# Two expert tiles per step, and TensorE's float32 work in six groups per turn

## The reference

```python
# 1 causal linear attention (4 heads of 64, 128 features), then a ReLU network
q, k = heads(x @ Wq) * dh**-.25, heads(x @ Wk) * dh**-.25; v = heads(x @ Wv)
qp, kp = phi(q), phi(k)          # exp(x@omega.T - |x|^2/2 - max)/sqrt(128) + 1e-6
attn = causal(qp @ kp.T) @ v / (row sums) @ Wo
h = layernorm_1e6(x + attn);  out = relu(h @ W1 + b1) @ W2 + b2      # 256 -> 1024 -> 256
# 2 cross attention, one head of 256, on a context of 256 rows
out = softmax((x@Wq.T + bq) @ (c@Wk.T + bk).T / 16) @ (c@Wv.T + bv)
# 3 mixture of experts: 16 experts, the best 2 for each row
gates = top2 of softmax(x @ Wg.T), normalised
out = sum_e gates[:, e] * ((silu(x @ W1[e]) * (x @ W3[e])) @ W2[e])     # 256 -> 176 -> 256
```

## Time and profile before

| | |
|---|---|
| median of 3 runs | 808.99 us (808.33 to 810.88) |
| the profiled execution | 809.31 us, of it 807.5 us from the first to the last instruction |
| PE / PEld busy | 98% / 93% of the span |
| DVE / ACT / POOL busy | 73% / 54% / 49% |
| turns 4 to 14 (the loop) | 143.25 to 546.00 us, 36.6 us each |
| tile stage | from 634.1 us (first row transpose) to the end |

### The profile page before, as it was taken

The page is one execution under the profiler, slowest core; times in us unless marked ns, Lnnn a source line. Parts: engine busy times, 40 slices in busy tenths (PEclk is TensorE's granted clock), DMA queues, the critical chain, the costliest instruction groups (busy, mean ns, idle before and its releaser), DMA issues. The chain is left out here.

```text
span 807.5 us, 20968 instructions
## 1 busy us (share of the span) xinstructions
PE 789.9 (98%) x5911; PEld 750.1 (93%) x5912; DVE 592.1 (73%) x1720; ACT 435.1 (54%) x1193; POOL 393.6 (49%) x560
## 2 busy tenths in 40 slices
PE   9999999999999999999999999999999999999995
PEld 8899999999999999999999999999897899999994
DVE  4757777888787878878887878778767566666663
ACT  4473554637273554547372644546255377767773
POOL 2432134443545344544445344544436368687886
PEclk9999999999999999999999999999999999999998
DMA  9786673755747392846657382849779458777780
GB/s 270 255 285 235 211 263 102 268 178 191 246 162 272 108 314 82 286 147 220 217 173 263 127 306 91 294 135 346 253 299 353 138 107 132 121 127 130 132 140 2
DMA packets 105962, 161.19 MB, mean 200 GB/s; under 512 B 10705, under 2 KB 69649, under 8 KB 105041
## 3 DMA queue, kind: packets, MB, share of 16 engines
q1 hardware_dynamic: 80544, 132.89, 48.0%
q0 software_dynamic: 14800, 17.61, 11.9%
q10 hardware_dynamic: 10576, 10.19, 4.9%
HBM read 50.14 MB, written 112.47 MB: 201 GB/s over the span
## 5 line engine op out<-in xcount | busy, mean ns | idle before, releaser
L799 POOL DMA_INDIRECT out<-narrow,sidx x79 | 122.8, 1554 | 45.4 <-DVE sidx L2043 23.3
L1274 ACT ACTIVATE xn3T<-ps 128x512 f32<-128x512 f32 (+1 forms) x18 | 10.3, 574 | 140.4 <-PE ps L819 135.9
L808 PE MATMUL ps<-w_hi,fT_hi 128*128 128x256 f32 x256 | 79.8, 312 | 0.2
L1339 ACT ACTIVATE phi<-ps,nmax 128x128 f32<-128x128 f32 x256 | 73.5, 380 | 8.1 <-DVE nmax L1745 7.9
L1601 DVE TENSOR_TENSOR fT_lo<-relu_v,fT_hi 128x512 fp32r<-128x512 f32 x64 | 51.1, 798 | 32.3 <-ACT relu_v L1353 32.3
L808 PE MATMUL ps<-w_hi,fT_lo 128*128 128x256 f32 x256 | 72.3, 282 | 0.0
L808 PE MATMUL ps<-w_lo,fT_hi 128*128 128x256 f32 x256 | 72.1, 282 | 0.0
L1353 ACT ACTIVATE relu_v<-ps,b_sb 128x256 f32<-128x256 f32 x128 | 68.9, 538 | 0.0
L1352 ACT ACTIVATE fT_hi<-ps,b_sb 128x256 fp32r<-128x256 f32 x128 | 67.9, 530 | 1.0 <-PE ps L808 1.0
L808 PE MATMUL ps<-hT_hi,w_hi 128*128 128x256 f32 x256 | 67.1, 284 | 0.0
L808 PE MATMUL ps<-hT_hi,w_lo 128*128 128x256 f32 x256 | 66.9, 283 | 0.0
(11 more groups left out here) (330 smaller groups left out, 2715.1 us busy)
## 6 DMA issues: line engine op xcount, KB each, us to landing
expert_rows<-zero_rows SPq DMA_DIRECT2D x16, 4352.0 KB, 16.2
narrow<-expert_rows ACTq DMA_DIRECT2D x71, 136.0 KB
expert_up_hi<-X SPq DMA_DIRECT2D x16, 352.0 KB, 2.8
e_hi<-expert_up_hi SPq DMA_DIRECT2D x2, 2816.0 KB, 10.1
part_raw<-in_E SPq DMA_DIRECT2D x30, 176.0 KB
expert_up_lo<-part_raw SPq DMA_DIRECT2D x15, 352.0 KB, 3.1
e_lo<-expert_up_lo SPq DMA_DIRECT2D x2, 2464.0 KB, 13.0
X<-in_x SPq DMA_DIRECT2D x16, 256.0 KB
```

Of the source, the lines that this page charges most:

```text
L799: pool.indirect_dma_start(out_rows, bass.IndirectOffsetOnAxis(sidx[:, u:u + 1], 0), yg[:, u, :], None, bounds_check=NT * P - 1, oob_is_err ...
L808: return pe.matmul(out_, lhsT, rhs, start=start, stop=stop)
L1274: return act.activation(out_, in_, ACT.Copy)
L1339: last = act.activation(phi[:, g, h, :], ps[:, g, h * M:(h + 1) * M], ACT.Exp, bias=nmax[:, g, h:h + 1])
```

## The change

In the turns: both halves of the q projection come first; context values are made in two halves around the transposes of xn2 (now into bank 2) and y, which thus stand together; `by_feature` waits first for xn2T_hi and later for xn2T_ready; counts, pr's transposes and half of phi's stand together behind the first half of `ffn_out`; the router stands before the last two steps of `ffn_out`, next to three other groups of transposes. ScalarE and VectorE swap hT before v2.

In the tile stage: a step takes two tiles. `in_pairs` replaces `in_groups`, and xgT gets four buffers. TensorE goes: turn_rows(s+4), turn_rows(s+5), turn_hidden(s), turn_hidden(s+1), up(s+2), up(s+3), down(s), down(s+1). The edges are turned before the first up. ScalarE's step reads two tile numbers first and loads tiles s+6 and s+7 behind both hidden_hi. `up` and `down` wait for the lo part at once.

```diff
-        xgT = tuple(sb(f"xgT_{part}", [P, 2, DC, P], F32R)[:, :, :, :] for part in ("hi", "lo"))
+        xgT = tuple(sb(f"xgT_{part}", [P, 4, DC, P], F32R)[:, :, :, :] for part in ("hi", "lo"))
...
+        def in_pairs(step, eng, begin=None):
+
+            for u in range(0, GB, 2):
+                step(u, u, 2, False)
+            with eng.Fori(0, (SLOT_TILES // GB - 2) // 2) as g:
+                if begin is not None:
+                    begin()
+                for u in range(0, 2 * GB, 2):
+                    step(g * 2 * GB + (GB + u), u % GB, 2, False)
+            if begin is not None:
+                begin()
+            for u in range(0, LEFT, 2):
+                step(SURE + u, u, min(2, LEFT - u), True)
+
+        def those_from(s, u, ahead, last):
+
+            return [(s + n, (u + n) % GB) for n in range(ahead, ahead + 2) if not (last and u + n >= LEFT)]
...
-            def by_feature(bank, srcT, w):
+            def by_feature(bank, srcT, w, rest_ready, value):
 
                 for e in range(DC):
+                    to = ps[:, bank, e * S:(e + 1) * S]
                     for c in range(DC):
-                        last = mm3(ps[:, bank, e * S:(e + 1) * S], w, srcT, cols(c, e * P, P), cols(c, 0, S),
-                                   c == 0, c == DC - 1)
+                        mm(to, w[0][cols(c, e * P, P)], srcT[0][cols(c, 0, S)], c == 0, False)
+                        mm(to, w[1][cols(c, e * P, P)], srcT[0][cols(c, 0, S)], False, False)
+                    if e == 0:
+                        pe.wait_ge(rest_ready, value)
+                    for c in range(DC):
+                        last = mm(to, w[0][cols(c, e * P, P)], srcT[1][cols(c, 0, S)], False, c == DC - 1)
                 return last
...
+                if a is not None and not first(a):
+                    project(1, wq)
                 if b is not None:
                     pe.wait_ge(ctx_ready, b + 1)
                     if not last_ffn:
-                        by_token(7, ctx, xwv).then_inc(v2_ps, 1)
+                        by_token(7, ctx, xwv, halves=range(1))
                     if not first(b):
                         pe.wait_ge(logit_ready, b)
                     if last_ffn:
                         keep_clock(0, 4)
                     pe.wait_ge(xn2_ready, b + 1)
-                    turn_tiles(6, xn2).then_inc(xn2T_ps, 1)
-                if a is not None and not first(a):
-                    project(1, wq)
+                    turn_tiles(2, xn2).then_inc(xn2T_ps, 1)
                 if last_ffn:
                     keep_clock(0, 1)
                 if f is not None:
                     pe.wait_ge(z_ready, f + 1)
                     turn_tiles(4, y).then_inc(zT_ps, 1)
                 if b is not None:
+                    if not last_ffn:
+                        by_token(7, ctx, xwv, halves=range(1, TS)).then_inc(v2_ps, 1)
                     if first(b):
                         pe.wait_ge(split_lo, N_DVE_SPLIT)
-                    pe.wait_ge(xn2T_ready, b + 1)
-                    by_feature(6, xn2T, xwq).then_inc(q_ps, 1)
+                    pe.wait_ge(xn2T_hi, b + 1)
+                    by_feature(6, xn2T, xwq, xn2T_ready, b + 1).then_inc(q_ps, 1)
...
-                if r is not None and not last_ffn:
-                    pe.wait_ge(v1_ready, a + 1)
-                    count_choices(r)
...
-                if f is not None:
-                    pe.wait_ge(fT_ready, f * 4 + 2)
-                    ffn_out(0, 0, FC // 2)
-                if b is not None:
-                    pe.wait_ge(pr_ready, b + 1)
-                    turn_tiles(7, pr).then_inc(prT_ps, 1)
-                if f is not None:
-                    pe.wait_ge(fT_ready, f * 4 + 4)
-                    ffn_out(0, FC // 2, FC)
-                if last_ffn:
-                    count_choices(r)
-                    ffn_out(1, 0, FC).then_inc(w2_ps, 1)
...
+                if f is not None:
+                    pe.wait_ge(fT_ready, f * 4 + 2)
+                    ffn_out(0, 0, FC // 2)
+                if r is not None and not last_ffn:
+                    pe.wait_ge(v1_ready, a + 1)
+                    count_choices(r)
+                if b is not None:
+                    pe.wait_ge(pr_ready, b + 1)
+                    turn_tiles(7, pr).then_inc(prT_ps, 1)
                 if a is not None:
+                    if f is not None:
+                        pe.wait_ge(relu_ready, f * 4 + 4)
                     turn_phi(0, qpT_ps)
+                if f is not None:
+                    pe.wait_ge(fT_ready, f * 4 + 4)
+                    ffn_out(0, FC // 2, FC)
+                if last_ffn:
+                    count_choices(r)
+                    ffn_out(1, 0, FC).then_inc(w2_ps, 1)
...
+                if b is not None and not last_ffn:
+                    router(b, 6)
                 if f is not None and not last_ffn:
                     ffn_out(1, FC - 2, FC).then_inc(w2_ps, 1)
-                if b is not None and not last_ffn:
-                    router(b, 6)
...
             def turn_rows(s, u):
+                if not (isinstance(s, int) and s < 2):
+                    pe.wait_ge(xgT_ready, s - 1)
                 pe.wait_ge(rows_loaded[u], (s - u) * PER + 16)
...
-                pe.wait_ge(xgT_hi, s + 1)
+                pe.wait_ge(xgT_ready, s + 1)
                 for c in range(DC):
                     part(0, e13_hi[:, c], c, c == 0, False)
                     part(0, e13_lo[c], c, False, False)
-                pe.wait_ge(xgT_ready, s + 1)
...
-                pe.wait_ge(hidT_hi, s + 1)
+                pe.wait_ge(hidT_ready, s + 1)
...
             keep_clock(2, 13)
             turn_rows(0, 0)
             turn_rows(1, 1)
+            pe.wait_ge(edges_loaded, 16 * 2)
+            for o in range(2):
+                last_mm = mm(ps[0:1, 7, o * P:(1 + o) * P], edge[:, o, D:D + 1], ident[:, :])
+            last_mm.then_inc(edge_ps, 1)
             up(0, 0)
-
-            def slot_tiles(s, u, last):
-                if isinstance(s, int) and s == 1:
-                    pe.wait_ge(edges_loaded, 16 * 2)
-                    for o in range(2):
-                        last_mm = mm(ps[0:1, 1, (2 + o) * P:(3 + o) * P], edge[:, o, D:D + 1], ident[:, :])
-                    last_mm.then_inc(edge_ps, 1)
-                if isinstance(s, int) and s == 3:
+            up(1, 1)
+            turn_rows(2, 2)
+            turn_rows(3, 3)
+
+            def two_tiles(s, u, n, last):
+                for v in those_from(s, u, 4, last):
+                    turn_rows(*v)
+                for k in range(n):
+                    turn_hidden(s + k, u + k)
+                for v in those_from(s, u, 2, last):
+                    up(*v)
+                if first(s):
+                    pe.wait_ge(e2_loaded, 16 * 3)
                     pe.wait_ge(edges_read, 1)
-                if not (last and u + 2 >= LEFT):
-                    turn_rows(s + 2, (u + 2) % GB)
-                if not (last and u + 1 >= LEFT):
-                    up(s + 1, (u + 1) % GB)
-                if isinstance(s, int) and s == 1:
-                    pe.wait_ge(e2_loaded, 16 * 3)
-                if not first(s):
-                    down(s - 1, (u - 1) % GB)
-                turn_hidden(s, u)
-
-            in_groups(slot_tiles, pe, expert_at.clear)
-            down(TILES - 1, LEFT - 1)
+                for k in range(n):
+                    down(s + k, u + k)
+
+            in_pairs(two_tiles, pe, expert_at.clear)
...
-            def slot_tiles(s, u, last):
-                if not (last and u + 2 >= LEFT):
-                    rows_hi(s + 2, (u + 2) % GB)
-                if not (first(s) or last):
-                    tile = tile_of(s + (GB - 1))
-                if not (last and u + 1 >= LEFT):
-                    gate_half(s + 1, (u + 1) % GB)
-                if not first(s):
-                    rows_out(s - 1, (u - 1) % GB)
-                hidden_hi(s, u)
-                if not (first(s) or last):
-                    load_rows(s + GB - 1, (u - 1) % GB, tile)
-
-            in_groups(slot_tiles, act)
-            rows_out(TILES - 1, LEFT - 1)
+            gate_half(1, 1)
+            rows_hi(2, 2)
+            rows_hi(3, 3)
+
+            def two_tiles(s, u, n, last):
+                loads = [] if first(s) else [(s + k, (u + k) % GB) for k in (GB - 2, GB - 1)
+                                             if not (last and u + k >= LEFT)]
+                tiles = [tile_of(v[0]) for v in loads]
+                for v in those_from(s, u, 4, last):
+                    rows_hi(*v)
+                for k in range(n):
+                    hidden_hi(s + k, u + k)
+                for v, tile in zip(loads, tiles):
+                    load_rows(*v, tile)
+                for v in those_from(s, u, 2, last):
+                    gate_half(*v)
+                for k in range(n):
+                    rows_out(s + k, u + k)
+
```

(65 more changed lines are left out.)

2 lines of the change are left out of this document (1 added, 1 removed).

## The result

| | before | after |
|---|---|---|
| median of the runs | 809.31 us (4 runs, 808.33 to 810.88) | 846.28 us (4 runs, 845.38 to 848.55) |
| ratio | | 1.0447, 95% interval 1.0424 to 1.0470 |
| span of the profiled execution | 807.5 us | 844.4 us |

What follows compares the result with a forecast made beforehand. TensorE was taken to set the pace in both stages. 809.3 - 1.5 (turns) + 22 (row loads) - 3 (pauses) + 2.1 (start) - 0.9 (end) = 828.0, or 827.5 us against the median; range 813 to 838.

Steps and rivals of the forecast that it cites:

- What bounds, and the switches: Both stages: TensorE sets the pace; a switch between float32 and float32r work costs 0, bound above 0.08 us.
- its two terms, -0.18 and +0.08 us a turn: Turns: the stall at phi's transposes goes (0.18 us); new waits at by_feature, router and xn3T cost 0.08; net -1.5 us.
- The steady state: Tile stage: 4.63 us from landing to landing against TensorE's 3.99, so it stands 0.64 us a step at turn_rows(s+5).
- the rival of a non-blocking wait: Tile stage: ScalarE's sequencer runs on to the loads, 4.49 us a step, total 823; chance 0.10.
- the term of 2.6 us: Tile stage: assumed landing time of a row load, taken between near loads of 2.2 and 3.1 us.
- the +22 us of the tile stage: Tile stage: TensorE's 0.64 us wait for row loads in each of 35 two-tile steps.
- The nearest row on the high side: Tile stage: a 352 KB load taking 3.1 us; as landing time it would give 35 x 1.14 = +40 us.
- the 2.3 us estimated from the Trainium skill: Tile stage: alternative landing time for 136 KB, about 2.0 us fixed plus bytes; would give 12 us in place of 22.
- The -3 us for TensorE's other pauses: Tile stage: gain taken because TensorE now stands at the loads anyway; -3 us (0 to -4).
- The lead of before: Tile stage of before: tile s+7 loaded in step s, turned in step s+5, 10 us later.
- The end: End of the tile stage: two 1.0 us waits become one, last scatter 5.2 to 5.4 us behind the last up; -0.9 us.
- The second chain: Tile stage: tile-number reads ahead of ScalarE's rounding delay down 0.2 us a step; not added. As rival (loads hidden) 815, chance 0.07.

Runs made afterwards that it cites:

- turns_only: The change's edits of the turns, on the tile stage of before: 808.32 us, ratio 0.9975 to before.
- phi_group_only: Before with one edit of the turns: counts, pr's transposes and half of phi's behind the first half of ffn_out; 808.20 us, ratio 0.9973.
- before_lead4: Before, one tile at a time, but step s loads tile s+4 in place of s+7: 865.97 us, ratio 1.0689.
- loads_first: After, but ScalarE issues both row loads behind the tile numbers and ahead of rows_hi and hidden_hi: 866.55 us, ratio 1.0677 to before.
- loads_behind_rows_out: After, but each row load goes out right behind the rows_out that frees its buffer: 846.70 us, ratio 1.0439 to before.
- rows_between: After, but turn_rows stands between up and down, with rows_hi and rows_in behind gate_half and product: 822.44 us, ratio 1.0144 to before.
- between_spread: rows_between, but with a tile number and a load behind each gate_half: 830.94 us, ratio 1.0264 to before.
- loads_on_sp: After, but SP issues the load of tile s+8 behind the release of scatter s, in ScalarE's place: 885.06 us, ratio 1.0928 to before.

## Why the prediction was right in kind and wrong in size

- **What bounds, and the switches**: held. The turns give -2 us (`turns_only`) for a forecast -1.5. Of its two terms, -0.18 and +0.08 us a turn, the first is -0.24 in the profile of `phi_group_only` and 2.2 us in its runs, for 2.5; the second is not shown, as said above.
- **The steady state**: the mechanism held, step by step: the wait is at turn_rows(s+5), a DMA ends it, and the blocking wait of ScalarE's sequencer gives 2.05 us from landing to issue for 2.03. The second load goes out behind the second `hidden_hi` and not behind the earlier rows_out, so the rival of a non-blocking wait is out. The Trainium skill (Perfetto Trace Analysis, section Sequencer Loop) says that the sequencer executes control instructions itself and puts engine instructions into a queue. The 2.05 us agree with it.
- **The step that failed is the size of the landing**, the term of 2.6 us, and with it the +22 us of the tile stage. The second loads take 2.90 in the mean of 35, the first ones 2.57. From T8 to T78 I had 143.6 + 22 - 3 = 162.6 us and it is 176.2, so 13.6 of the 18.2 us that the sum lacks are here. They can be told apart along the cycle: 34 times 0.25 us, 9 in all, since the 34 second loads behind the first take 2.85; 3 us since the way from a landing to the next issue is 2.12 in the mean and not 2.03 (its longest are 3.21 and 2.78, both among the first four, just behind the stretch at the lower clock); and 2 us at the first wait, 2.9 where I had 0.64 a step.
- **The range** ended at 838 for a landing of 2.9 us. With that landing the sum still lacks 3 us of the way to the next issue, 2 at the first wait, 2 of the turns (1.5 of them at the lower clock), 2 at the end and 0.5 at the start. The nearest row on the high side, 3.1 us with its +40, I had left outside the range.
- **Page and measurement**: the 2.3 us estimated from the Trainium skill (DMA: Bandwidth & Descriptors, section Anatomy of one DMA) would have given 12 us. The measurement decides against it here: the shortest landing in after is 2.03 us and the mean 2.73.
- **The -3 us for TensorE's other pauses**: no run shows this gain. In before the tops of three passes stand out by 0.27 to 0.37 us each (the `up` at 685.66, 718.47 and 751.52), 1.0 us together; in the one at 685 TensorE's sequencer reads an expert's number for 0.30 us. All that is late before `up` and `down` is 3.6 us in before and 6.7 in after, 1.5 of it by the clock.
- **The lead of before**: I had 10 us from a load's issue to its transposes; it is 7.3 (before_lead4 and its expectation showed the miscount of a step). It entered no term.
- **The end**: -0.9 for +1.0. I followed the data to the last product and not GpSimd's queue behind it, though I had its 1.86 us.
- **The second chain**: 0.2 forecast, 0.28 measured once the loads are out of the way. "Gives way to the first" was right for this kernel, but I held the two apart. They share ScalarE's control work, some 1.7 us a step, and `loads_first` and `loads_behind_rows_out` show that moving it turns one chain's loss into the other's.

What stays open: why a second load takes longer than a first; the last 0.2 us a step of `rows_between` over before's 4.10 (ScalarE's control work by its trace, but no order that I tried removed it); and what the start of the stage loses. That `up` and `down` now wait for the lo part at once was not run alone.

The best kernel measured is `phi_group_only` (`turns_only` equals it): the tile stage of before with one edit of the turns, 0.27% under before.

## What to carry to other kernels

When a loop body is doubled, count for each load the time from its issue to its first use and not the buffers: here the same eight buffers gave 7.3 us before and 1.3 after, and a landing of 2.6 to 2.9 us then set the pace. Price a load twice, by its landing and by the control work that its issue puts ahead of the engine's next instruction; and add up what the issuing engine does for each load, 3.05 us on SP here, before giving it the work. Gathering float32 work for its own sake won nothing here, since a switch costs 0.08 us at one end and gives it back at the other.

## What the hardware showed that I had not expected

Two loads of 136 KB issued 0.66 us apart from one queue did not land alike: 2.57 us for the first and 2.90 for the second in after, 2.13 and 2.94 in `loads_first`, 2.35 and 3.02 in `rows_between`. Issued 1.15 us apart in `loads_behind_rows_out`, both took 2.2 to 2.3. But the distance does not settle it: in `between_spread` they go out 1.17 us apart and take 2.55 and 2.97. The scatters' traffic lies differently in these kernels too; the cause is not shown.

An issuing engine can also be the limit by its control work alone, with every semaphore met: SP needed 3.05 us for each tile in `loads_on_sp`, though its loads landed 2.1 us (median) behind their issue, sooner than those of ScalarE in after.
